# Batch 0's attention and the feed-forward in one program, batch 0 in halves of two tiles

## The reference, cut to what matters

```python
# image attention, for each batch (x after the experts; k_v is ctx_512, 512 x 128)
kv   = k_v @ W_k.T + b_k                      # 512 x 128, needed as it is and transposed
out  = layernorm(x) @ kv                      # 512 x 128
sim  = (out @ kv.T) * scale                   # 512 x 512
sim  = (sim - mean) * rsqrt(var + eps) * ln_gamma + ln_beta
x    = x + softmax(sim)
# feed-forward
h    = silu(layernorm(x) @ w_gate) * (layernorm(x) @ w_up)     # 2048 hidden columns
h    = keep the two largest in magnitude of every four
x    = x + h @ w_down
```

## Time and profile before

| | before |
|---|---|
| median of 3 runs | 1099.79 us (1099.70 to 1102.07) |
| profiled execution: time | 1100.21 us |
| profiled execution: span | 1098.5 us |
| TensorE busy in the span | 969.8 us (88%) |
| VectorE busy | 667.2 us (61%) |
| ScalarE busy | 390.1 us (36%) |
| GpSimd busy | 299.9 us (27%) |
| mean granted TensorE clock | 0.93 |

### The profile page before, as it was taken

How to read it: one execution, slowest core, us unless ns; L and a number is a source line. 1 busy time by engine, 2 the same in 40 slices (tenths; PEclk the granted TensorE clock), 3 DMA queues, 4 the chain that set the end, 5 groups by cost and what they waited for, 6 DMA issues and landing times.

```text
span 1098.5 us, 15596 instructions
## 1 busy us (share of the span) xinstructions
PE 969.8 (88%) x4615; PEld 804.8 (73%) x4616; DVE 667.2 (61%) x1436; ACT 390.1 (36%) x681; POOL 299.9 (27%) x368
## 2 busy tenths in 40 slices
PE   4996539999999996427598999999999999999997
PEld 3883339999999995316477788888888888888886
DVE  7986734432445223683479697885786858664446
ACT  4875334322445222222343353242432333221221
POOL 0465023341232402221453443131320411101120
PEclk8998759999999997567888999999999999999999
DMA  8268144452444312304764743475343672344751
GB/s 329 67 147 211 39 159 153 158 177 83 150 167 138 95 57 85 125 10 165 293 236 174 281 154 129 166 247 167 105 149 131 197 225 77 115 156 156 225 137 55
DMA packets 64155, 167.32 MB, mean 152 GB/s; under 512 B 7648, under 2 KB 7776, under 8 KB 62944
## 3 DMA queue, kind: packets, MB, share of 16 engines
q0 software_dynamic: 28160, 79.71, 24.4%
q1 hardware_dynamic: 35936, 86.88, 22.2%
HBM read 118.59 MB, written 47.98 MB: 152 GB/s over the span
## 4 chain that ended last, share of the span: by engine, by line
PE 38%; DVE 10%; POOL 2%; ACT 2%; DMA 1%; issue 1%; ACTq 0%; DVEq 0%; POOLq 0%
PE ps L77 13%; PE ps L79 13%; PE ps L78 13%; DVE raw L2555 3%; DVE f_hid L2571 1%; DVE x L2590 1%; PE ps L2160 1%; DMA raw<-in_ffn_gu 1%; POOL f_w L1439 1%; DVE kv_c_lo L2577 1%; POOL f_w L1444 1%; DVE l_stats L2223 0%; DVE x L2213 0%; DVE x L2272 0%; DVE kv_c_raw L2263 0%
## 5 line engine op out<-in xcount | busy, mean ns | idle before, releaser
L77 PE MATMUL ps<-f_x_lo,f_w 128*128 128x512 f32 x512 | 205.5, 401 | 9.3 <-POOL f_w L1439 4.2
L78 PE MATMUL ps<-f_x_hi,f_w 128*128 128x512 f32 x512 | 204.2, 399 | 0.0
L79 PE MATMUL ps<-f_x_hi,f_w 128*128 128x512 f32 x512 | 203.9, 398 | 0.0
L1494 DVE TENSOR_TENSOR f_hid<-moe_rows,ps 128x512 f32<-128x512 f32 x64 | 43.9, 686 | 139.6 <-PE ps L79 107.6
L77 PEld LDWEIGHTS ps<-f_x_lo,f_w 128*128 128x128 f32 x512 | 98.3, 192 | 33.4 <-POOL f_w L1439 4.9
L79 PEld LDWEIGHTS ps<-f_x_hi,f_w 128*128 128x128 f32 x512 | 98.3, 192 | 22.5
L78 PEld LDWEIGHTS ps<-f_x_hi,f_w 128*128 128x128 f32 x512 | 98.3, 192 | 21.9
L77 PE MATMUL ps<-gu_w_lo,m_xT_hi 128*128 (+1 forms) x312 | 106.3, 341 | 5.1 <-DVE m_xT_lo L1735 5.0
L1488 ACT ACTIVATE moe_rows<-ps 128x512 f32<-128x512 f32 x64 | 38.2, 596 | 202.9 <-PE ps L79 202.9
L77 PE MATMUL ps<-f_w,kv_c_hi 128*128 128x512 f32 x256 | 102.2, 399 | 2.3 <-DVE x L2590 2.3
L79 PE MATMUL ps<-gu_w_hi,m_xT_hi 128*128 (+1 forms) x312 | 101.9, 327 | 0.0
(11 more groups left out here) (354 smaller groups left out, 1918.8 us busy)
## 6 DMA issues: line engine op xcount, KB each, us to landing
f_w<-w_scratch POOLq DMA_DIRECT2D x36, 1024.0 KB, 6.1
f_w<-w_scratch POOLq DMA_DIRECT2D x36, 512.0 KB, 5.6
w_scratch<-f_w SPq DMA_DIRECT2D x16, 1024.0 KB, 7.8
raw<-in_moe_gu SPq DMA_DIRECT2D x32, 352.0 KB, 4.2
y_scratch<-m_y SPq DMA_DIRECT2D x39, 256.0 KB, 2.3
raw<-in_ffn_gu SPq DMA_DIRECT2D x16, 512.0 KB, 5.5
w_scratch<-f_w SPq DMA_DIRECT2D x16, 512.0 KB, 4.1
raw<-in_moe_dn SPq DMA_DIRECT2D x24, 256.0 KB
```

What stands on the lines that cost most here:

```text
L77: eng.matmul(out, lhs_hi, rhs_lo, start=start, stop=False)
L78: eng.matmul(out, lhs_lo, rhs_hi, start=False, stop=False)
L79: return eng.matmul(out, lhs_hi, rhs_hi, start=False, stop=stop)
L1494: dve.tensor_tensor(out, sg[:, k % 2, :], self.up_bank(n, r), ALU.mult).then_inc(self.hid_made, 1)
```

## The change

`image_attention` goes, and a class `First` takes its place. Its streams stand at the head of the feed-forward's streams, in one block, with no barrier between. All gate/up weight buffers are allocated from the start; the keys of batch 0 and its context product lie in the third of them, `w[2]`, so the cast into it waits for the last similarity. Batch 0 goes through the attention in two halves of two tiles, which alternate with one another and with the keys of batches 1 to 3. SyncE issues the first four raw loads at once. ScalarE casts the first two weights between the keys. GpSimd does the low half of a weight between the steps of the attention. Behind that, ScalarE casts the fourth weight after silu(0,0), and `pre(6)` and `early(6)` stand ahead of the selection of unit 0. The instructions themselves are those of before, but for statistics, pow and `nmean` by halves and six matmul groups on 256 columns.

```diff
-image_attention(nc, outer, dram)          # a block of its own
-ffn(nc, outer, dram, out)
+ffn(nc, outer, dram, out)                 # with First's streams at its head
...
+class First:
+        self.first = [u.w[2][:, part, 0:2, :].rearrange("p k n -> p (k n)") for part in range(2)]
+        self.o_hi, self.o_lo = (u.w[2][:, part, 2, :] for part in range(2))
...
+    def sync(self, sp):
+        u, dram = self.u, self.dram
+        for name in ("gamma", "beta"):
+            sp.dma_start(self.keys[name][:, :], dram[name].broadcast_to([P, N])).then_inc(self.ld_row, 16)
+        for r in range(2):
+            u.load_gate_up(sp, dram["ffn_gu"], 0, r)
+        for r in range(2):
+            u.load_down(sp, dram["ffn_dn"], 0, r)
...
+    def pool(self, pool):
...
+        for j in range(2 * TB):
+            pool.indirect_dma_start(out=self.pair[j], ...).then_inc(self.fetched[j], 16)
+        rstd(0, 0)
+        u.pool_gate_up(pool, 0, 0)
+        rstd(0, 1)
+        later.fetch(pool, 0, 0)
+        rs(0)
+        rs(1)
+        rs(2)
+        rs(3)
+        rstd(1, 0)
+        u.pool_gate_up(pool, 0, 1)
+        rstd(1, 1)
+        later.fetch(pool, 0, 1)
...
+    def pe(self, pe):
...
+        key_product(0); key_turn(0)
+        key_product(1); key_turn(1)
+        key_product(2); key_turn(2)
+        turn(0, 0)
+        key_product(3)
+        context(0)
+        similar(0)
+        key_turn(3)
+        turn(0, 1)
+        context(1)
+        similar(1)
+        turn(1, 0)
+        turn(1, 1)
+        pe.wait_ge(self.lo_done[1], TB)
+        u.pe_gate_up(pe, 0, 0)
...
+    def act(self, act):
...
+        for b in range(3):
+            kvT_hi(b)
+            kv_hi(b)
+            if b < 2:
+                u.act_gate_up(act, 0, b)
+        norm(0)
+        hi(0, 0)
+        kvT_hi(3)
+        o_hi(0)
+        kv_hi(3)
+        norm(1)
+        hi(0, 1)
+        o_hi(1)
+        for t in range(TB):
+            exp(t)
+        hi(1, 0)
+        hi(1, 1)
...
+    def dve(self, dve, chain):
...
+        def add(t):
+            for k in range(2):
+                dve.wait_ge(self.fetched[2 * t + k], 16)
...
+        kvT(0); key_lo(0)
+        kvT(1); add(0); key_lo(1); add(1)
+        stats(0, 0)
+        kvT(2); add(2); key_lo(2); add(3)
+        dve.wait_ge(self.ld_row, 32)
+        lo(0, 0)
+        stats(0, 1)
+        kvT(3)
+        o_lo(0)
+        centre(0); centre(1)
+        lo(0, 1)
+        scores(0); scores(1)
+        key_lo(3)
+        o_lo(1)
+        prob(0); centre(2); prob(1); centre(3)
+        stats(1, 0)
+        scores(2); scores(3)
+        fnorm(0)
+        prob(2); prob(3)
+        lo(1, 0)
+        stats(1, 1)
+        self.later.dve_add(dve, 0, 0)
+        fnorm(1)
+        lo(1, 1)
...
 # ffn, SyncE, GpSimd, TensorE
+                first.sync(sp)
                 gate_up_round(0)
+                first.pool(pool)
                 for r in range(2, RQ):
+                first.pe(pe)
                 for r in range(1, RQ):
...
 # ffn, ScalarE
+                first.act(act)
+                act.wait_ge(first.sim_done, TB)
+                u.act_gate_up(act, 0, 2)
                 for r in range(1, RQ):
-                    if r >= 2:
-                        u.act_gate_up(act, 0, r)
                     early(r)
                     u.act_silu(act, 0, r - 1, sg)
+                    if r == 1:
+                        u.act_gate_up(act, 0, 3)
                     late(r)
                 for r in range(RQ - 1):
                     u.act_gate_up(act, 1, r)
                 u.act_silu(act, 0, RQ - 1, sg)
+                early(6)
                 size(0, 0)
...
 # ffn, VectorE
+                first.dve(dve, chain)
                 hidden(0, 0)
                 for r in range(1, RQ):
                     pre(r)
                     hidden(0, r)
                     post(r)
+                pre(6)
                 keep_two(0, 0)
                 keep_two(0, 1)
                 for n in range(1, UNITS):
-                    pre(6 * n)
+                    if n >= 2:
+                        pre(6 * n)
                     split(n - 1, 0)
                     hidden(n, 0)
```

More of the change, by code:

```diff
@@ L2298, in sb @@
             return ctx.enter_context(nc.sbuf_tensor("f_" + name, shape, dt))
-        u, later = outer["units"], outer["later"]
-        u.x_hi.append(sb("x_hi1", [P, DC, N], F32R))
-        u.x_lo.append(sb("x_lo1", [P, DC, N], F32R))
-        for r in range(2, RQ):
-            u.add_weights(sb(f"w{r}", [P, 2, 3, D], F32R))
+        outer["keys"] = {
+            **{name: sb("k_" + name, [P, B - 1, 2 * N], F32R) for name in ("hi", "lo")},
+            **{name: sb("k_" + name, [P, N]) for name in ("gamma", "beta")},
+        }
+        w = [sb(f"w{r}", [P, 2, 3, D], F32R) for r in range(RQ)]
+        x_hi, x_lo = ([sb(f"{name}{k}", [P, DC, N], F32R) for k in range(2)] for name in ("x_hi", "x_lo"))
+        u = outer["units"] = Units("f_", outer, w, x_hi, x_lo)
+        later = outer["later"] = Later(sb, outer)
         hid_hi, hid_lo = (outer["kv"][name][:, :].rearrange("p (r n) -> p r n", r=RQ) for name in ("c_hi", "c_lo"))
@@ L2309, in ffn @@
         hid = sb("hid", [P, RQ, N])
+        first = First(sb, outer, dram, hid)
         mag = outer["kv"]["c_raw"][:, 0:2 * N].rearrange("p (r n) -> p r n", r=RQ)
@@ L2685, in build @@
             experts.close()
-            with ExitStack() as last:
-                def sb_last(name, shape, dt=F32):
-                    return last.enter_context(nc.sbuf_tensor(name, shape, dt))
-                outer["keys"] = {
-                    **{name: sb_last("k_" + name, [P, B - 1, 2 * N], F32R) for name in ("hi", "lo")},
-                    **{name: sb_last("k_" + name, [P, N]) for name in ("gamma", "beta")},
-                }
-                x_hi, x_lo = ([sb_last(f"f_{name}0", [P, DC, N], F32R)] for name in ("x_hi", "x_lo"))
-                w = [sb_last(f"f_w{r}", [P, 2, 3, D], F32R) for r in range(2)]
-                outer["units"] = Units("f_", outer, w, x_hi, x_lo)
-                outer["later"] = Later(sb_last, outer)
-                image_attention(nc, outer, dram)
-                ffn(nc, outer, dram, out)
+            ffn(nc, outer, dram, out)
 def kernel(x, ctx_512, L0_xattn_W0, L0_xattn_a_self0, L0_xattn_a_neigh0, L0_xattn_b0, L0_xattn_W1,
```

473 lines of the change are left out of this document (218 added, 255 removed).

## The result

| | before | after |
|---|---|---|
| median (4 runs each) | 1099.74 us (1099.15 to 1102.07) | 1088.88 us (1086.76 to 1091.23) |
| profiled execution: time | 1100.21 us | 1088.75 us |
| profiled execution: span | 1098.5 us | 1087.1 us |
| TensorE busy | 969.8 us | 964.4 us |
| mean granted TensorE clock | 0.93 | 0.935 |

The ratio is 0.9898, with an interval of 0.9873 to 0.9923: faster by 10.9 us. The forecast was 1090.0, in a range of 1080.5 to 1097.5. Its time, its side and its likeliest case came true. Its parts did so less well: in this profile part 1 gave less and part 2 more, both partly by TensorE's clock, and 2 to 3 us come from something that no part of the sum had.

A forecast was written before the change was run, and what follows sets the result against it. TensorE's stream from 598.60 on was taken as the bound, with VectorE's order deciding before the first gate/up matmuls. Terms 6.8 + 3.0 + 0.3 = 10.1 us off 1100.21 gave 1090.1, stated as 1090, range 1080.5 to 1097.5.

The forecast's parts named there:

- likeliest case: Whole kernel: the forecast itself, 1090 us, with a range of its own of 1086 to 1094; chance 0.58.
- part 1: Head, attention of batch 0 by halves: VectorE's gaps shrink, first gate/up matmuls start 6.8 us earlier.
- part 2: Behind the first gate/up matmuls, one program without barrier: earlier raw loads bring the selection forward, 3.0 us gained.
- S: Start of the first gate/up matmuls, 499.62 before; forecast at 492.8, with 490 to 496 as sign.
- gathers later by 2 us: Head: the early raw loads share bandwidth and delay the row gathers by 2 us, bounds 0 and 4.
- nothing on balance: Head: GpSimd's subtractions slow VectorE by 2.0 and 1.5 us, instead of 1.9 and 1.7 before.
- The half of (1,0): Behind S: GpSimd's weight half ends at S+25.65 instead of S+27.9, 2.25 us gained, releasing raw load (1,2).
- slow first half: Selection of unit 0: its first group keeps taking 4.06 us on VectorE under GpSimd's subtraction.
- Part 3: o_lo ahead of the selection: the 11.7 us wait goes, but the first score of batch 1 gains only 0.3 us.
- TensorE as the pace: Rival, behind S: 6.8 and the 11.7 us of o_lo are both gained, giving 1081 us; chance 0.16.
- The front giving nothing: Rival, head: raw loads hold ScalarE, S stays near 499.6, only 3.3 us gained, giving 1096.5 us; chance 0.17.
- The casts ahead of the keys costing more: Rival, head: late loads make the casts cost more than all else gains, 1103 if landing at 455; chance 0.09.

The follow-up runs named there:

- rs_early: Changed kernel with GpSimd's two rs of batch 1 moved ahead of the last two down halves of unit 0 and of (2,0); 1087.00 us, ratio 0.9877.
- silu_first: Changed kernel with silu(0,3), o_hi and the first size ahead of ScalarE's cast (1,2); 1087.51 us, ratio 0.9880.
- rs_and_gather_early: Changed kernel with GpSimd's rs of batch 1 and the next half batch's gathers ahead of the same down halves; 1085.96 us, ratio 0.9855.
- raw_late: Changed kernel with the third and fourth raw loads held until the first gate/up product is done, ScalarE's casts ordered as before; 1092.80 us, ratio 0.9908.
- locks_moved: Changed kernel with GpSimd's low halves (0,0) and (0,1) moved to where VectorE reads PSUM or waits; 1085.51 us, ratio 0.9845.
- before_o_lo_early: Kernel before, with only o_hi and o_lo of batch 1's first half moved ahead of the selection of unit 0; 1100.88 us, ratio 1.0000.
- o_lo_late: Changed kernel with o_hi and o_lo of batch 1's first half put back behind the selection of unit 0; 1089.17 us, ratio 0.9884.
- after_again: The changed kernel run once more, with no edit; 1087.32 us, ratio 0.9883.
- all_five: Changed kernel with GpSimd's head halves moved, raw loads behind gathers, casts behind o_hi(0), rs and gathers early, and silu(0,3) first; 1080.98 us, ratio 0.9824.
- before_both_early: Kernel before, with both o_lo and GpSimd's rs of batch 1 moved early; 1099.13 us, ratio 0.9977.
- casts_behind_keys: Changed kernel with ScalarE's casts (0,0) and (0,1) both behind the keys of batch 1, raw loads as they are; 1087.49 us, ratio 0.9868.

## Why the prediction was right, point by point

**What bounds.** Right: S came earlier and the time followed, and nothing that was only a wait inside (11.7 us for `o_lo`) is in the time. The smaller moves behind S, 1.8 to 2.9 us of hidden(2,0) in rs_early, silu_first and rs_and_gather_early, do not stand out of the noise of the medians, so for them it is not shown.

**Part 1, forecast 6.8.** The profile after shows 4.2, the five other profiles with the same head show 6.4 to 6.7. Between them stands TensorE's clock at the first similarities (last section), which no edit set. Before, the four similarities ran at the higher clock, as in these five; so the five are the closer comparison, and part 1 is worth 6.4 to 6.7 by them. The forecast, though, walked with similarities at the lower clock (two in 2.8 us), and at that clock it was 2.6 us too good: S - T0 of 63.84 against 61.2. That it meets the five is in part luck, as this error and the higher clock cancel. The terms that were mis-sized are "gathers later by 2 us", where VectorE waited 3.6, and "nothing on balance" for GpSimd's halves: 2.0 and 1.5 us of lock were reckoned, 2.05 and 2.04 found (3.65 against 1.60, 2.78 against 0.74), together 2.2 of the 2.6. The Trainium skill (DMA: Bandwidth & Descriptors, section Queues, rings and completion order) has the engines go round the queues that have work; the forecast set it aside as not shown by a row. The wait of 2.96 us for a gather, and 0.2 in all with the raw loads behind the gathers, agree with it, as they would with any other way of sharing the engines.

**GpSimd against VectorE.** The Trainium skill (SBUF — State Buffer, section Who interferes with whom) names VectorE instructions with two SBUF inputs as those locked out. 3.65 against 1.60 and 2.78 against 0.74 agree. The `nmean` of 2.14 us in rs_early, a `tensor_scalar`, has one SBUF input, of 2 elements a row, and was held too. The same section exempts a single SBUF input only outside VectorE's two-port modes, and names `tensor_scalar` among the instructions that can enter them, so this does not speak against it. No run shows which mode it ran in; two BATCH_NORM_AGGREGATE under the same subtraction took 0.25 us together and were not held.

**Part 2, forecast 3.0.** The two profiles show 4.8, of which 1.3 is the earlier rise of the clock. At like clock it is 3.3 to 3.6, and raw_late undoes 3.2 to 3.5. The half of (1,0) was to end at S+25.65 and ends at S+25.9 in locks_moved (GpSimd's 514.70 plus 2.40; S+24.6 in the profile after, with the clock). One term was too large: the raw load behind it lands for its cast after 5.9 us (520.64 to 526.50) and not 6.6: 0.7 us more of gain, less 0.25 for the half. The "slow first half" of the selection was misplaced, at no cost: its first group takes 1.90 us and not 4.06, as GpSimd's subtraction begins only at 531.60, but the next instruction then takes 2.38 us and not 0.29.

**Part 3, forecast 0.3.** Right in the medians of two runs, and within 0.2 to 0.4 us by the traces (0.5 to 0.7). What ends the chain is rs on GpSimd, 5.90 us, as said; behind it the gathers, and then the selection.

**The term that was left out.** From hidden(2,3) to the last hidden tile no instruction changed, and the stretch is 450.67 us and not 453.85. TensorE has no wait in it in either profile, and the full clock throughout. It is 453.70 in before_o_lo_early, also without a wait. It is 451.64 in o_lo_late, 451.50 in after_again and 451.45 in all_five, each with one wait of 0.4 to 0.5 us, and 455.28 in before_both_early, with waits of 1.0. Every sixth matmul of TensorE's timeline before, around 816, where the product with w[1] ends and that with w[2] begins:

```profile
812.85 0.39 PE L79 MATMUL ps<-f_x_hi,f_w 128*128 128x512 f32 x1
...
814.21 0.39 PE L79 MATMUL ps<-f_x_hi,f_w 128*128 128x512 f32 x1
...
815.57 0.40 PE L79 MATMUL ps<-f_x_hi,f_w 128*128 128x512 f32 x1
...
816.97 0.40 PE L79 MATMUL ps<-f_x_hi,f_w 128*128 128x512 f32 x1
...
818.37 0.40 PE L79 MATMUL ps<-f_x_hi,f_w 128*128 128x512 f32 x1
```

Six matmuls take 1.36 us up to 815.57, which is 0.2267 each, and 1.40 behind it, 0.2333 each, at the same clock and with the same operands of x: only the weight buffer is another. Before, the gate/up products of w[0] and w[1] have the wide spacing (0.2333) in the units of batches 1 and 3 and the narrow one for batch 2, and w[2] and w[3] the other way round: wide is a pair of buffers that were allocated in different blocks. In the changed kernel all come from one place, and every gate/up product of the stream has the narrow spacing. The down matmuls go the other way: six take 1.40 us in every case after, and before 1.40 with w[0] and w[1] but 1.37 to 1.39 with w[2] and w[3], 1.389 on the mean of both. From unit 3 on that is 624 gate/up matmuls times 0.0067 won, 4.2 us, less 624 down matmuls times 0.0019, 1.2: 3.0, where the profiles without a wait show 3.0 to 3.2, and those with one 2.1 to 2.4. In the layout of the two programs the gate/up pairs with the narrow spacing are those in which both buffers start at the same byte modulo 64, and those with the wide one are 32 apart. The quick pairs are equal modulo 4096 too, so the modulus is not told. This was read off two layouts; no run shifted a buffer to try it, and the down matmuls follow it only in part. The diff showed the moved allocations; the prediction counted instructions and waits, and not where operands lie.

**The sum.** In the profiled executions: T0 0.6 later, part 1 4.2 (with some 2.5 lost to the clock), part 2 4.8 (with 1.3 won by it), to hidden(2,0) another 0.8 (of which the first score 0.3), to hidden(2,3) 1.0 lost as one wait became two (2.32 and 3.45) and the clock fell at 598.57, and 3.2 in the stream: 11.4. The forecast had 10.1 with nothing in the stream. Without the 2 to 3 us of the layout it would have been 1 to 2 us too good, well inside its range. That it is within 1.3 us is luck in part: part 1 was 2.6 too good, the earlier clock behind S and the layout gave 1.3 and 3.2 that stand in no term, the lost wait took 1.0, and these nearly cancel.

**The signs.** S was to come at 490 to 496 and came at 496.04; the first score at S+62 to S+64, and it came at S+61.1, or S+62.6 at like clock. ScalarE waits for raw twice, 3.15 us at 439.55 and 0.45 at 442.05. TensorE's last long waits are 4.17, 2.32 and 3.45, each under the 5 that would have spoken against it.

**The rivals.** TensorE as the pace (1081) is out: 10 to 12 us of wait for `o_lo`, added or taken away, move hidden(2,0) by 0.5 to 1.4. The front giving nothing (1096.5) is out by S. The casts ahead of the keys costing more is out by casts_behind_keys, where they cost nothing that shows (0.03 us).

## What to carry to other kernels

A wait of 11.7 us on the engine that bounds is worth what the next thing in line allows; walk the other engines' queues to the point where the stream runs free, and price that. Put large transfers behind small ones that someone waits for, and a GpSimd pass over SBUF under VectorE work that reads PSUM or waits anyway: here those two moves gave 5.1 us of 1087.49 within one group of runs, nearly half of what the whole rewrite gave. Before two profiles are compared stage by stage, look at where the clock rose in each. When a change moves allocations, compare the spacing of the same matmuls in both traces: 3% of the rate of a product lay in which buffers it read.

## What the runs showed of the hardware

TensorE's clock at the same instructions differs from execution to execution. At the first similarity the changed kernel's two profiles, the first from the run after and the second from after_again, with the same gaps ahead of them:

```profile
459.60 0.79 PE L77 MATMUL ps<-f_w 128*128 128x512 f32 x1 [0.92 <-DVE f_w L2254]
460.19 0.63 PE L78 MATMUL ps<-f_w 128*128 128x512 f32 x1
```

```profile
461.20 0.50 PE L77 MATMUL ps<-f_w 128*128 128x512 f32 x1 [0.92 <-DVE f_w L2254]
461.54 0.39 PE L78 MATMUL ps<-f_w 128*128 128x512 f32 x1
```

The kernel before, at one of its first similarities:

```profile
469.74 0.50 PE L77 MATMUL ps<-a_first_lo,a_o_hi 128*128 128x512 f32 x1 [1.40 <-DVE a_o_lo L2053]
470.07 0.39 PE L78 MATMUL ps<-a_first_hi,a_o_lo 128*128 128x512 f32 x1
```

A matmul of 512 columns takes 0.63 us where the granted clock is 0.50 (1.2 GHz) and 0.39 where it is 1.00 (2.4 GHz). With the higher one already there S - T0 is 61.3 to 61.6 (five profiles of the unchanged head), with the lower 63.8 (two): 2.3 us that belong to no edit, a third of part 1. A difference of that size between two single profiles says nothing of an edit; it needs the medians. Two more such differences: T0, ahead of which no experiment changed anything, lies between 431.06 and 434.53 in the fourteen profiles. And the stretch from the last hidden tile to the end takes 29.6 to 29.8 us where the granted clock fell in it (at 1076.2 in the profile after) and 28.2 where it stayed up to the last microsecond (after_again), with either kernel.

What stays open: whether the offset of two operands modulo 64 sets the spacing of matmuls or another property of the two layouts does, and so whether hidden halves moved by 32 bytes would quicken the 768 down matmuls, by at most 768 times 0.0067, 5 us, an estimate. And why the moves behind S, which at like clock bring hidden(2,0) forward by 2.6 us (silu_first) and 2.9 (rs_and_gather_early), are within the noise of the medians.
